# Second mixture of experts: the first layer made channel by channel from copied expert matrices, its bias added on ScalarE

## What is computed

```python
gate_scores = x @ Wg + bg
top1 = jnp.argmax(gate_scores, axis=-1)
onehot = jax.nn.one_hot(top1, Wg.shape[-1], dtype=x.dtype)
h = jax.nn.relu(jnp.einsum('btd,edh->beth', x, W1) + b1[None, :, None, :])
y = jnp.einsum('beth,ehd->betd', h, W2) + b2[None, :, None, :]
out = jnp.einsum('betd,bte->btd', y, onehot)
```

## Time and profile before

| | before |
|---|---|
| runs, us | 3095.9, 3096.38, 3113.73 (median 3096.38) |
| profiled execution, us | 3111.27 |
| its span, first to last instruction, us | 3109.8 |
| mean granted TensorE clock | 0.873 |
| busy: PE / DVE / ACT / POOL | 83% / 72% / 67% / 40% |
| last phase | from 2878 us, 232 us |
| its slot loop | from 2971 us |

### The profile page before, as it was taken

One profiled execution on the slowest core, in us unless ns is written; L12 is line 12 of the kernel. 1 busy time (PEld: TensorE's weight loads), 2 busy tenths in 40 slices (PEclk: granted clock), 3 DMA queues, 4 the chain that ended last, 5 costly groups with the idle time before them and its releaser, 6 DMA issues. The chain is left out here.

```text
span 3109.8 us, 68711 instructions
## 1 busy us (share of the span) xinstructions
PE 2589.3 (83%) x19758; PEld 1312.1 (42%) x19758; DVE 2228.3 (72%) x8194; ACT 2086.2 (67%) x3430; POOL 1253.6 (40%) x1598
## 2 busy tenths in 40 slices
PE   7958888888888888658786699999999999999278
PEld 5725555555555555435321133332333333333245
DVE  8638777777777787447456899898988889991322
ACT  5749878888888888525221188787877878889022
POOL 1427767777777777523002422222222223000432
PEclk9968889888888888889787599999999999999589
DMA  7720000000000000181531133233323333210221
GB/s 230 257 65 11 13 14 12 12 12 12 22 12 14 12 12 12 38 268 31 85 85 48 54 85 93 86 93 93 84 85 90 88 101 98 71 46 2 90 72 45
DMA packets 159444, 205.97 MB, mean 66 GB/s; under 512 B 74511, under 2 KB 127053, under 8 KB 159081
## 3 DMA queue, kind: packets, MB, share of 16 engines
q1 hardware_dynamic: 148732, 161.85, 19.2%
q0 software_dynamic: 10352, 39.92, 3.7%
HBM read 135.21 MB, written 66.62 MB: 65 GB/s over the span
## 5 line engine op out<-in xcount | busy, mean ns | idle before, releaser
L2143 ACT ACTIVATE pb<-sps 128x512 f32<-128x512 f32 (+1 forms) x1664 | 894.0, 596 | 281.1 <-PE sps L2085 266.9
L2166 DVE TENSOR_REDUCE mx<-wps 128x2 f32<-128x802 f32 x1024 | 954.1, 989 | 94.9 <-PE wps L2058 79.5
L1076 DVE MAX8 cand<-sc 128x8 f32<-128x46 f32 (+1 forms) x4480 | 603.2, 199 | 181.3 <-issue 112.3
L852 PE MATMUL scores<-ctxT,qT 97*128 97x512 f32 (+1 forms) x1024 | 486.2, 629 | 94.5 <-ACT sc L964 81.5
L2100 PE MATMUL ops<-pb,va 128*9 128x256 f32 x6656 | 529.1, 389 | 9.4 <-ACT ot L2149 8.4
L852 PEld LDWEIGHTS scores<-ctxT,qT 97*128 97x128 f32 x1024 | 224.9, 229 | 370.8 <-issue 271.1
L1942 POOL COPY va<-XX 128x128 f32<-128x128 f32 (+1 forms) x208 | 50.2, 299 | 705.7 <-PE ops L2100 697.9
L735 POOL TENSOR_TENSOR prf<-sc,prf 128x1601 f32<-128x1601 f32 x64 | 229.7, 3589 | 150.2 <-ACT prf L971 149.0
L2058 PE MATMUL wps<-FO,Y 56*128 56x401 bf16 x1024 | 196.8, 369 | 49.1 <-DVE mx L2166 34.0
L735 POOL TENSOR_TENSOR prs<-sc,prs 128x1601 f32<-128x1601 f32 x64 | 230.4, 3600 | 10.1 <-ACT prs L971 5.0
L827 PE MATMUL misc<-diag,prs 128*128 128x128 f32 (+1 forms) x1664 | 229.1, 292 | 5.5 <-issue 4.5
(11 more groups left out here) (411 smaller groups left out, 4073.7 us busy)
## 6 DMA issues: line engine op xcount, KB each, us to landing
FO<-keys SPq DMA_DIRECT2D x392, 50.0 KB
XX<-keys SPq DMA_DIRECT2D x392, 50.0 KB
keys<-kpb POOLq DMA_DIRECT2D x42, 400.2 KB, 3.5
toep<-kernpad SPq DMA_DIRECT2D x8, 2048.0 KB, 15.1
values<-s_vs SPq DMA_DIRECT2D x16, 832.0 KB, 6.0
XX<-values SPq DMA_DIRECT2D x16, 832.0 KB, 4.5
keysf<-s_kf SPq DMA_DIRECT2D x16, 800.5 KB, 3.9
Y<-queries SPq DMA_DIRECT2D x784, 8.0 KB
```

What stands on the lines that cost most here:

```text
L852: ins = t.matmul(scores[:, c:c + n], q, ctxT[par][0:C + 1, c:c + n], start=True, stop=True)
L1076: st.add(v.max(cand[s % 2][:, 8 + n:8 + n + 7 * NP + 1:NP], sc[s % 4][:, c:c + w]))
L2143: nc.scalar.activation(pb[(UNITS * g + u) % 8][0:rows_, :, :], sps[(UNITS * g + u) % SB][0:rows_, :, :], ACT.Exp).then_inc(p_ready, 1)
L2166: v.tensor_reduce(mx4[:, q, h:h + 2, c], both, AX.X, ALU.max).then_inc(work_read, 1)
```

## The change

- The first layer of a slot is made channel by channel. Instead of one product with the tokens as rows (128 tokens x 512 columns) there are four, each giving 128 hidden channels as rows and the 128 tokens as columns. The result already lies as the second layer needs it, so `turn_hidden`, its PSUM tiles e_ht, the tile e_hr and DVE's copy e_hrT go.
- The stationary operand is now the expert's matrix. DVE copies it for each slot from e_w1 into one of two tiles e_w1s, and the expert's bias column into e_b1s. This is `slab(s)`: it waits until the activation of slot s - 2 is done, reads the expert's number on DVE, and makes two copies. `slab(0)` and `slab(1)` run ahead of the loop; in the loop `slab(s + 2)` stands ahead of `finish(s)`.
- ACT applies the relu with the bias, four activations of 128x128 a slot, straight into e_hrT.
- b1 is loaded by channel (e_b1T, 128x8x4) as the last of the weight loads; its cutting into three parts on POOL, its six small DMAs and the bias product go.
- The gate's weights and bias have a semaphore of their own, g_in. TensorE no longer waits for the experts' matrices ahead of the gate, but only behind it.

```diff
+            def slab(s):
+
                 if s >= 2:
-                    dve.wait_ge(y_ready, s - 1)
-                v.tensor_copy(hrT[s % 2][:, :, :], ht[s % 2][:, :, :]).then_inc(hrT_ready, 1)
+                    dve.wait_ge(hrT_ready, s - 1)
+                e = dve.value_load(whoi[0:1, s:s + 1], min_val=0, max_val=E - 1)
+                v.tensor_copy(b1s[s % 2][:, :], b1T[:, bass.ds(e, 1), :].rearrange("p o c -> p (o c)")).then_inc(slab_ready, 1)
+                v.tensor_copy(w1s[s % 2][:, :], w1[:, bass.ds(e, 1), :].rearrange("p o h -> p (o h)")).then_inc(slab_ready, 1)
+
+            dve.wait_ge(w_in, 16 * 3)
+            slab(0)
+            slab(1)
...
             for s in range(SLOTS):
-                dve.wait_ge(x_in[s % XB], nth(s, XB))
-                turned(s)
-                if s:
-                    finish(s - 1)
-            finish(SLOTS - 1)
+                if s + 2 < SLOTS:
+                    slab(s + 2)
+                finish(s)
...
-            pe.wait_ge(w_in, 16 * 4)
...
             begin(0)
+            pe.wait_ge(g_in, 16 * 2)
...
-            pe.wait_ge(halves_in, 32)
+            pe.wait_ge(w_in, 16 * 3)
+            pe.wait_ge(halves_in, 16)
...
-            def first(s, e):
+            def first(s):
                 pe.wait_ge(xT_ready, s + 1)
+                pe.wait_ge(slab_ready, 2 * s + 2)
                 if s >= 2:
                     pe.wait_ge(hrT_ready, s - 1)
+
                 for c in range(4):
-                    ins = t.transpose(ht[s % 2][:, c, :], hr[s % 2][:, c * P:c * P + P], ident[:, :])
-                ins.then_inc(ht_ready, 1)
+                    ins = t.matmul(hp[s % 2][:, c * P:c * P + P], w1s[s % 2][:, c * P:c * P + P], xT[s % 2][:, :],
+                                   start=True, stop=True)
+                ins.then_inc(h_ready, 1)
...
-                s_.activation(hr[s % 2][:, :], hp[s % 2][:, :], ACT.Relu).then_inc(hr_ready, 1)
+                    act.wait_ge(y_ready, s - 1)
+                for c in range(4):
+                    ins = s_.activation(hrT[s % 2][:, c, :], hp[s % 2][:, c * P:c * P + P], ACT.Relu,
+                                        bias=b1s[s % 2][:, c:c + 1])
+                ins.then_inc(hrT_ready, 1)
```

More of the change, by code:

```diff
@@ L2236, in mixture1_phase @@
         w2 = sb("e_w2", [P, E, 4, D])
-        b1, b2 = sb("e_b1", [E, HID]), sb("e_b2", [E, D])
-        b1h = [sb(f"e_b1h{n}", [E, HID], BF16) for n in range(3)]
+        b1T, b2 = sb("e_b1T", [P, E, 4]), sb("e_b2", [E, D])
+        w1s, b1s = [sb(f"e_w1s{i}", [P, HID]) for i in range(2)], [sb(f"e_b1s{i}", [P, 4]) for i in range(2)]
         b2h = [sb(f"e_b2h{n}", [E, D], BF16) for n in range(3)]
-        b1p, b2p = sb("e_b1p", [3, E, HID], BF16), sb("e_b2p", [3, E, D], BF16)
+        b2p = sb("e_b2p", [3, E, D], BF16)
         one3 = sb("e_one3", [3, P], BF16)
@@ L2264, in mixture1_phase @@
         xT = [sb(f"e_xT{i}", [P, P]) for i in range(2)]
-        hr = [sb(f"e_hr{i}", [P, HID]) for i in range(2)]
         hrT = [sb(f"e_hrT{i}", [P, 4, P]) for i in range(2)]
@@ L2269, in mixture1_phase @@
         hp = [ps(f"e_hp{i}") for i in range(2)]
-        ht = [ps(f"e_ht{i}", (P, 4, P)) for i in range(2)]
         yp = [ps(f"e_yp{i}") for i in range(2)]
         X, ident = k.X, k.ident
-        lgp, locp, cntp = hp[0], hp[1], ht[0]
-        w_in, bias_in, consts = sem("e_w_in"), sem("e_bias_in"), sem("e_consts")
+        lgp, locp, cntp = hp[0], hp[1], yp[0]
+        g_in, w_in, bias_in, consts = sem("e_g_in"), sem("e_w_in"), sem("e_bias_in"), sem("e_consts")
         halves_ready, halves_out, halves_in = sem("e_halves_ready"), sem("e_halves_out"), sem("e_halves_in")
@@ L2295, in _ @@
         def _(sp):
[L2296 to L2299, removed]
+            sp.dma_start(b2[:, :], a["L1_ffn_b2"]).then_inc(bias_in, 16)
+            for dst, src in ((wg[:, :], a["L1_ffn_Wg"]), (bg[:, :], a["L1_ffn_bg"].partition_broadcast(P))):
+                sp.dma_start(dst, src).then_inc(g_in, 16)
+            for dst, src in ((w1[:, :, :], a["L1_ffn_W1"].rearrange("e d h -> d e h")),
                              (w2[:, :, :, :].rearrange("p e c d -> p (e c) d"),
-                              a["L1_ffn_W2"].rearrange("e (c p) d -> p (e c) d", p=P))):
+                              a["L1_ffn_W2"].rearrange("e (c p) d -> p (e c) d", p=P)),
+                             (b1T[:, :, :], a["L1_ffn_b1"].rearrange("e (c p) -> p e c", p=P))):
                 sp.dma_start(dst, src).then_inc(w_in, 16)
@@ L2342, in _ @@
             pool.sem_inc(rows_ready, 1)
[L2343 to L2348, removed]
+            pool.wait_ge(bias_in, 16)
+            for n in range(3):
+                st.link(g_.tensor_copy(b2h[n][:, :], b2[:, :]))
+                if n < 2:
+                    st.link(g_.tensor_tensor(b2[:, :], b2[:, :], b2h[n][:, :], ALU.subtract))
             pool.sem_inc(halves_ready, 1)
@@ L2389, in _ @@
             dve.wait_ge(consts, 1)
-            dve.wait_ge(w_in, 16 * 4)
+            dve.wait_ge(g_in, 16 * 2)
             dve.wait_ge(lg_ready, NG)
@@ L2407, in _ @@
             dve.wait_ge(loc_ready, 2)
-            cnt = cntp[:, 0, 0:E]
+            cnt = cntp[:, 0:E]
             st.link(v.tensor_tensor(more[:, :, :], over(cnt, T), rows(steps[:, :], E), ALU.is_gt))
@@ L2475, in _ @@
             o = locp[:, 0:T * E]
-            t.matmul(cntp[:, 0, 0:E], all1[:, :], total[:, T - 1, :], start=True, stop=True).then_inc(loc_ready, 1)
+            t.matmul(cntp[:, 0:E], all1[:, :], total[:, T - 1, :], start=True, stop=True).then_inc(loc_ready, 1)
             t.matmul(o, before[:, :], ohb[:, :, :].rearrange("p j e -> p (j e)"), start=True, stop=False)
@@ L2523, in _ @@
                 e = expert(s)
-                first(s, e)
+                first(s)
                 if s:
                     second(s - 1, last)
-                turn_hidden(s)
                 if s + 2 < SLOTS:
@@ L2593, in flamingo_kernel @@
         k.sorted = dram("sorted", [SLOTS * P, ROW])
[L2594 removed]
+        k.b2p = dram("b2p", [3, E, D], BF16)
         with ExitStack() as layer0:
```

21 lines of the change are left out of this document (4 added, 17 removed).

## The result

After the change the program takes 3054.75 us, the median of 3041.88, 3053.55, 3055.95 and 3057.19. The kernel before, run beside it, has 3096.14 (four runs, 3094.37 to 3113.73). The ratio of the times is 0.9845, with an interval of 0.9800 to 0.9890: faster by 11 to 20 parts in 1000.

What follows compares the result with a forecast made beforehand. TensorE was taken to bound the last phase's slot loop. Savings of 24.8 (slots), 1.4 (opening), 1.6 (end) and 1.8 us (ahead), minus 0.3, make 29.3 us less: 3067.1 us against the median 3096.38, range 3061 to 3079.

Steps and rivals of the forecast that it cites:

- A slot on TensorE: Last phase's loop: a slot's products sum to 2.45 us (bounds 2.30 and 2.52) instead of 3.14, 24.8 us less over 36 steps.
- The step that failed: Slot loop: the new first layer's four float32 products priced at 1.09 us, like the second layer's four; bounds 0.96 and 1.14.
- The loop's opening: First slots of the loop, TensorE at half clock: slot 2 starts near 2980.0 instead of 2981.44, 1.4 us less.
- The loop's end: From slot 38's first layer to the last e_ob: 3.9 us instead of 5.52, 1.6 us less.
- Ahead of the loop: Phase's opening: without POOL's 8x512 splitting, DVE's second row-scaling group takes about 1.7 us instead of 3.52, 1.8 us less.
- The 0.3 put in for copies holding up the scatter: Ahead of the loop: copies for slots 0 and 1 delay the scatter by at most 0.9 us; 0.3 us counted as loss.
- The separate wait for the gate's weights: Ahead of the gate: waiting for its weights alone removes a wait covered from 2895.51 to 2896.6, so by itself gains nothing.
- The load's price of 16 us: New e_b1T load of 4096 single values: lands 16 us behind the large weights, near 2912, needed only at 2972.9.
- Rival 1: Slot loop: DVE's copy of the expert's matrix comes late and sets the slot, time 3073 to 3082 us; chance 0.2.
- Rival 2: Slot loop: TensorE's sequencer limits, register reads of about 0.86 us staying on the path, time 3078 to 3085 us; chance 0.06.
- Rival 3: Slot loop: TensorE's clock stays at half, a slot takes 4.9 us, 63 us more, time 3155 us; chance 0.04.
- ACT and DVE keep up: Slot loop: four activations take 1.07 to 1.47 us; DVE's copy ends at 4.3 us, wanted at 4.90, margin 0.6 or 0.3.

Runs made afterwards that it cites:

- b_rows128: Kernel before with both bias products padded from 3 rows to 128, the added rows zero: mean slot step 3.034 us against 3.142, last phase 227.2 us against 231.6.
- a_split1: Changed kernel with POOL's loading and three-part cutting of the 8x512 hidden bias put back, result unused: gate at 39.41 us against 37.67, step 2.199, phase 192.8.
- a_win: Changed kernel with TensorE again waiting for all weights ahead of the gate: gate at 40.31 us against 37.67, phase 194.6 us against 191.7.
- a_resid2: Changed kernel with DVE adding the output bias to the residual rows instead of TensorE, two e_w1s buffers: step 1.923 us against 2.199, phase 180.7 against 191.7.
- a_rows128: Changed kernel with the output bias product padded from 3 rows to 128 with zeros: step 1.976 us against 2.199, phase 183.6 us against 191.7.
- a_nob2: Changed kernel without the output bias product on TensorE, that bias left out: step 1.928 us against 2.199, phase 181.7 us against 191.7.
- a_resid3: Changed kernel with DVE adding the output bias to the residual rows instead of TensorE, three e_w1s buffers: phase 179.8 us, whole program 3042.6 us, ratio 0.9839.
- b_nob1: Kernel before without the hidden layer's bias product on TensorE, that bias left out: mean step 2.816 us against 3.142, phase 219.1 us against 231.6.

## Why the prediction came out as it did

It had said that it is wrong if the slot is not 2.45 us, and there it is wrong. Step by step:

- **A slot on TensorE: mechanism right, size wrong.** TensorE stayed the bound, and the slot is the sum of its products, as said. But it is 2.20, below the lower bound of 2.30. Three terms of the sum were off: the first layer, 0.89 for 1.09; the second layer, 0.99 for 1.09; bias and turn behind it, 0.32 for 0.27. Together 0.25 x 36 = 9.0 us, nearly all of the 10.6 us by which the forecast of 29.3 missed.
- **The step that failed** is "the second layer is made of exactly four such and takes 1.09 us, and I take that". The 1.09 were read from start to start in a place between two few-row products. They held 0.89 of its own, 0.10 for the passage from the hidden bias's 3 rows to 128 rows, which shows up between its first two halves, and 0.10 for the passage to the output bias; with both bias products at 128 rows (b_rows128) the same four products take 0.89. The new first layer stands behind a 128-row turn and ahead of a 128-row product, and the second layer stands behind it: they have none of the first kind. That taking off a few-row product gives more than its duration, I missed as well. The lower bound was no bound either: 0.96 for the wide layer held the passage into its bias, 0.10 of the same kind (0.43 us from its first half to its second, 0.53 from that to the bias).
- **It could have been read in the trace of before**, in a place far from the loop. A product of 128x128 float32 with a 1-row bias product of the same type behind it, in the timeline of before:

```profile
1422.96 0.29 PEld L1634 LDWEIGHTS bank<-b,ones 1*128 1x128 f32 x2
1422.96 0.48 PE L1634 MATMUL bank<-b,ones 1*128 1x128 f32 x2
1423.37 0.97 PEld L1633 LDWEIGHTS bank<-w,gl 128*128 128x128 f32 x8
1423.37 1.16 PE L1633 MATMUL bank<-w,gl 128*128 128x128 f32 x8
```

  Two halves with one row take 0.41 us from start to start, and eight with 128 rows take 1.16 with an end that is modelled 0.28 behind the last start: 0.88 for seven intervals, one of them 0.21 and the others 0.11.
- **The loop's opening: 2.7 less, 1.4 forecast.** The layers priced at half clock had the same fault: the first two took 1.84 (2941.67 to the turn at 2943.51) and 1.71 where 2.2 each were put in, the third 1.85 for 2.2. The clock's rise shows in the windows above, near 2947.3. The opening is 4.7 to 6.1 us in the seven kernels derived from after.
- **The loop's end: 1.5 less, 1.6 forecast.** Right. (I had counted from the first layer's load, 0.11 ahead of its product.)
- **Ahead of the loop: 1.7 less, 1.8 forecast.** The second group took 1.77 (forecast 1.7) and the gate moved by 1.70, and a_split1 takes exactly that back. Right, and shown. Here the Trainium skill, page "SBUF — State Buffer", section "Who interferes with whom", has VectorE and GpSimd share a port pair that one of them holds for a whole instruction; the trace agrees, with 3.52 beside the splitting of 8x512 and 1.77 beside that of 8x128. The 0.3 put in for copies holding up the scatter did not show: the loop moved by 1.67, the gate by 1.70.
- **The separate wait for the gate's weights "by itself gives nothing": right against the old loads, wrong in the changed kernel.** Its new last load, e_b1T, took 11.3 us to issue and lands 17.3 us from the start of its issue, 20.0 after the phase began. Behind the wait as it was, it would have cost 2.6 us (a_win). The load's price of 16 us was near; that it would run beside the large matrices and not behind them, I had not seen.
- **Rival 1, the copy comes late: shown not to be so; in the changed kernel it is the store that waits.** The copy takes 0.43 us beside POOL's store as without it, and even at a slot of 1.92 it is in time (a_resid2). The store alone takes 0.982 us. Where it starts well behind the copy and runs into it by more than 0.13, it ends 0.855 us behind the copy's end: in after the overlap is 0.14 us and the store takes 0.998 in the median of 33, in a_rows128 0.24 and 1.097, in a_nob2 0.30 and 1.157, as the timeline of a_nob2 has it:

```profile
3001.01 0.43 DVE L2427 COPY e_w1s<-e_w 128x512 f32 x1
3001.13 1.16 POOL L2356 DMA_INDIRECT out_dram<-e_ob,e_xs  x1 [0.73 <-issue]
```

  So all but these stores' first 0.13 us stood still for the copy. It isn't always so. In a_resid3, where the copy mostly begins only some 0.02 us ahead of the store, it is the copy that grows, to 0.48 in the median, and the store keeps its 0.982:

```profile
3000.28 0.48 DVE L2414 COPY e_w1s<-e_w 128x512 f32 x1 [0.83 <-DVE e_ob L2433]
3000.31 0.98 POOL L2342 DMA_INDIRECT out_dram<-e_ob,e_xs  x1 [0.92 <-DVE e_ob L2433]
```

  And where the store begins first, by 0.07 us (two stores of after) up to 0.24 (two each in a_rows128 and a_nob2), neither grows. By the Trainium skill, page "SBUF — State Buffer", section "Who interferes with whom", one of the two has to stand still for the other's whole instruction; this trace agrees for the stores that begin well behind the copy, and not for these others, which ran beside it. Why is open. The store's buffers hide its wait, as the prediction had held possible, and nobody in the loop waits for it.
- **Rival 2, the sequencer: not in the changed kernel.** TensorE is busy 40.00 of 40.00. The register way was near the bound in the old kernel, though (b_nob1, b_rows128), which I had not priced.
- **Rival 3, half clock: no.** 1.00 throughout the loop.
- **ACT and DVE keep up: right.** Four activations take 1.14 (bounds 1.07 to 1.47). DVE's chain of read, bias column and matrix ends 1.35 us into the following slot, 3.55 behind the start of its own, where 4.3 were forecast. The shorter slot wants it at 4.41.
- **The sum.** 33.9 + 2.7 + 1.5 + 1.7 = 39.8 us, against 39.9 measured. Nothing of size is left over.

## What to carry to other kernels

A duration read from start to start belongs to a product and its neighbours. Before such a price is used in another place, see what stands ahead of it and behind it, above all whether a stationary operand of few rows is next to it. A product with few rows, a bias with a row of ones, costs much more than its columns: padded with zeros to 128 rows it costs 0.04 us here instead of 0.29. And when products are taken from a busy engine, look for the second and third longest way through the slot, for they decide how much of it arrives.

## What the runs showed of the hardware

- **A stationary operand of few rows.** Between products of 128 rows the load of the next runs under the present one: halves of a float32 product follow at 0.11 us at a granted clock of 1.00 (2.4 GHz). When 128 rows are followed by 3 or by 1, the load starts 0.20 us behind the start of the last product and the product follows 0.20 instead of 0.11 behind; the passages back add 0.10 and then 0.05 or another 0.10. It isn't the number format: the 1-row product is float32 and shows the same. Why the load isn't taken ahead, no run here shows. The Trainium skill, page "TensorE: Matmul & The Clock Gate", section "Step-by-step: what each phase is for", says that loads are pulled ahead of running products when their row groups don't conflict or when they go to the background buffer, and that the row count doesn't matter for a load's time. The rows agree that the load itself isn't longer (0.09 for 3 rows, 0.10 for 128), and show that it starts late.
- **A change of the row count alone is not it.** In an early phase of the kernel before, at a granted 1.00, products of 97, 128 and 96 rows follow one another with no passage, five in 0.56 us and four in 0.43:

```profile
39.15 0.72 PE L300 MATMUL ps_s<-wv,s_ctxT 97*128 97x128 f32 x5
39.71 0.60 PE L293 MATMUL ps_s<-ident,s_ctxn 128*96 128x128 f32 x4
40.14 0.22 PE L297 MATMUL ps_s<-s_ctxT,wk 96*128 96x65 f32 x1
```

  So do 128, 65 and 97 rows (L835 and L852, 0.11 each time). A product of 8 rows (L1681) starts 0.525 behind a 512-column half of 128 rows (L1688), as the 3-row bias does, and not 0.43. Where between 8 and 65 rows the border lies, no clean pair here shows. Few rows are not the only such case: a product whose stationary operand has 128 rows but a single column (L860) starts 0.205 or more behind a half of 128 columns (L827) in all 62 cases, where 0.11 is usual.
- **A register read is a long way on TensorE**: 0.85 us from the start of the read to the start of the product that uses it (b_nob1), and 0.72 on DVE from read to copy, of which the load is 0.30.
- **Four activations with a bias column** of 128x128 follow one another every 0.26 us (1.14 for four); a copy of that shape without a bias takes 0.27 on ACT.
- **4096 single values** hold SP's queue for 11.3 us, and are in SBUF 17.3 us from the start:

```profile
L2300 SPq DMA_DIRECT2D e_b1T<-in_L_ffn_b_dram x1: 11319/11319/11319, 2851.4 to 2851.4; - x1
...
DMA to landing us min/median/max: 17.3/17.3/17.3
```
